# Four scatters of a batch in one run ahead of the masking products, in place of two pairs around them

## What is computed

```python
h = _layernorm(x) * (1 + ca) + sa
x = x + ga * attention(h)          # 16 heads of 8 columns, windows of 64 tokens
h = _layernorm(x) * (1 + cb) + sb
x = x + gb * experts(h)            # 8 experts, hidden 352, the best 2 of each token

# attention: a window of 64 queries sees its own 64 keys (causal) and the 64 before it
scores = einsum('bhcqd,bhckd->bhcqk', qc, kcat) / HD ** 0.5
attn = softmax(where(mask, scores, -inf))
out = einsum('bhcqk,bhckd->bhcqd', attn, vcat) @ w_out
# experts
top_vals, top_idx = top_k(xt @ Wg.T, 2)
y = W2[e] @ (silu(W1[e] @ t) * (W3[e] @ t)), weighted by softmax(top_vals), summed over the two
```

## Time and profile before

| | |
|---|---|
| time, median of 3 runs | 276.14 us (273.75 to 278.57) |
| profiled execution | 275.3 us |
| its span, first to last instruction | 273.1 us |
| granted PE clock, mean over the span | 0.932 of full speed |
| PE busy | 218.6 us (80%), 2696 instructions |
| DVE busy | 166.8 us (61%) |
| ACT busy | 115.3 us (42%) |
| POOL busy | 126.6 us (46%), 125 instructions |
| POOL, scatters into `routed` (L1392) | 32 instructions, 32.4 us |
| POOL, masked keys (L1381) | 7 instructions, 16.2 us |

### The profile page before, as it was taken

One profiled execution on the slowest core, in us unless ns is written; L12 is line 12 of the kernel. 1 busy time (PEld: TensorE's weight loads), 2 busy tenths in 40 slices (PEclk: granted clock), 3 DMA queues, 4 the chain that ended last, 5 costly groups with the idle time before them and its releaser, 6 DMA issues.

```text
span 273.1 us, 7726 instructions
## 1 busy us (share of the span) xinstructions
PE 218.6 (80%) x2696; PEld 149.7 (55%) x2698; DVE 166.8 (61%) x527; ACT 115.3 (42%) x259; POOL 126.6 (46%) x125
## 2 busy tenths in 40 slices
PE   6875998999989899997688875698999999993000
PEld 2442465756546575664456654476778887872000
DVE  4695599998585968858472944633444444442492
ACT  3324455546554544654435331223444444433430
POOL 5727263508549183764224174523444444444251
PEclk9999799999999999999979995979999999999555
DMA  6329900000000010000101121231121111100851
GB/s 185 108 79 431 447 23 2 4 2 22 22 13 29 2 33 12 22 22 13 31 22 58 31 60 48 69 88 59 58 60 57 48 52 43 58 21 31 265 159 38
DMA packets 16488, 19.32 MB, mean 71 GB/s; under 512 B 2578, under 2 KB 14998, under 8 KB 16202
## 3 DMA queue, kind: packets, MB, share of 16 engines
q1 hardware_dynamic: 13786, 14.43, 16.6%
q0 software_dynamic: 2240, 4.28, 4.5%
q10 hardware_dynamic: 432, 0.20, 0.3%
HBM read 13.03 MB, written 6.13 MB: 70 GB/s over the span
## 4 chain that ended last, share of the span: by engine, by line
PE 59%; DVE 16%; DMA 6%; ACT 6%; issue 4%; another core or an unknown queue 2%; POOL 2%; SPq 1%; ACTq 0%; DVEq 0%; POOLq 0%
PE pair L754 9%; PE pair L728 7%; PE pair L730 7%; PE pair L560 4%; PE pair L539 4%; DVE nd L1010 4%; ACT pt L841 4%; PE pair L736 4%; PE pair L504 4%; PE pair L545 3%; PE pair L575 3%; PE pair L476 2%; DVE fin_b L1330 2%; PE pair L534 2%
## 5 line engine op out<-in xcount | busy, mean ns | idle before, releaser
L1440 POOL DMA_INDIRECT ranked<-y_sb,ix_u x36 | 35.4, 984 | 46.5 <-ACT y_sb L930 35.9
L1306 DVE TENSOR_TENSOR gated<-pair,act 128x352 f32<-128x352 f32 x36 | 18.9, 524 | 51.8 <-PE pair L730 41.8
L841 ACT ACTIVATE pt<-pair 128x1024 f32<-128x1024 f32 x32 | 33.0, 1030 | 31.7 <-PE pair L545 31.7
L1010 DVE TENSOR_REDUCE nd<-pair 128x8 f32<-128x1024 f32 x32 | 37.7, 1220 | 9.4 <-PE pair L504 9.1
L1392 POOL DMA_INDIRECT routed<-pay,row_u x32 | 32.4, 1012 | 12.6 <-issue 6.3
L754 PE MATMUL pair<-we_sb,gated_t 128*128 x216 | 31.9, 286 | 0.8 <-ACT y_sb L930 0.8
L728 PE MATMUL pair<-we_sb,x_t 128*128 x72 | 29.7, 495 | 2.8 <-ACT x_t L924 2.8
L754 PEld LDWEIGHTS pair<-we_sb,gated_t 128*128 128x128 f32 x216 | 28.2, 199 | 1.7 <-issue 1.6
L730 PE MATMUL pair<-we_sb,x_t 128*128 x72 | 28.2, 474 | 0.0
L1357 POOL TENSOR_TENSOR rstd<-veps,cf_sb 128x2 f32<-128x2 f32 x8 | 6.0, 748 | 47.5 <-DVE veps L1050 47.5
L914 ACT ACTIVATE act<-pair 128x352 f32<-128x352 f32 x36 | 16.7, 464 | 16.0 <-PE pair L728 16.0
(11 more groups left out here) (167 smaller groups left out, 388.1 us busy)
## 6 DMA issues: line engine op xcount, KB each, us to landing
we_sb<-we SPq DMA_DIRECT2D x1, 4352.0 KB, 18.9
xt_in<-routed SPq DMA_DIRECT2D x36, 64.5 KB
mod_bc<-mod_rows SPq DMA_DIRECT2D x1, 2048.0 KB, 8.7
fin_y<-ranked SPq DMA_DIRECT2D x8, 256.0 KB, 4.7
out<-fin_b SPq DMA_DIRECT2D x8, 128.0 KB, 1.8
x_all<-x SPq DMA_DIRECT2D x1, 768.0 KB, 6.2
ranked<-y_sb,ix_u POOLq DMA_INDIRECT x36
routed<-pay,row_u POOLq DMA_INDIRECT x32
```

What stands on the lines that cost most here:

```text
L841: act.activation(pt[:, 2 * half:2 * half + 2, :].rearrange("p j k -> p (j k)"), src[:, :], ACT.Exp).then_inc(done, 1)
L1010: dve.tensor_reduce(nd[:, :, 2 * half:2 * half + 2, 0].rearrange("p s j -> p j s"), src[:, :].rearrange("p (j s k) -> p j s k", j=2, s=4), ...
L1440: pool.indirect_dma_start(ranked[:, :], bass.IndirectOffsetOnAxis(ap=ix_u[q][:, 0:1], axis=0), y_sb[q][:, :], None, bounds_check=TOPK * TO ...
```

## The change

In iterations 3 to 7 POOL first waits until the scores of unit 2b + 1 are done, then issues all four scatters of batch b - 3, and then does the two masking products. The scatters at the end of the iterations go away, and behind the loop the four scatters of batch 5 go out without a wait on `pv_done`. Nothing else changes; PE, DVE, ACT and SP have the same instructions in the same order.

```diff
             for b in range(B):
+                if b >= 3:
+                    pool.wait_ge(s_done, 2 * b + 2)
+                    rows_chosen(b - 3)
+                    scatter_tile(b - 3, 0)
+                    scatter_tile(b - 3, 1)
                 if b + 1 < B:
                     mask_k(b + 1)
-                if b >= 3:
-                    pool.wait_ge(pv_done, 2 * b)
-                    scatter_tile(b - 3, 1)
-                if b + 1 < B:
                     mask_q(b + 1)
...
                 if b >= 1:
                     inv_std2(b - 1)
-                if b >= 2:
-                    rows_chosen(b - 2)
-                    scatter_tile(b - 2, 0)
                 gate_wout(b)
-            pool.wait_ge(pv_done, G)
+            rows_chosen(B - 3)
+            scatter_tile(B - 3, 0)
             scatter_tile(B - 3, 1)
             inv_std2(B - 1)
```

## The result

The changed kernel takes 302.64 us (median of 4 runs, 301.22 to 305.19), the kernel before beside it 275.41 us: a ratio of 1.104, with a 95% interval of 1.098 to 1.110. I had predicted 276.9 us and no measurable difference. It is slower by about 27 us. The profiled execution took 301.2 us, its span (first to last instruction) 299.0 us against 273.1.

What follows compares the result with a forecast made beforehand. The prediction took a chain on PE, then DVE, to bound each attention period, without POOL. Only L1068's delay counted, 4 x 0.18 = 0.72 us, other terms zero: 276.14 + 0.72 = 276.9 us, range 274.3 to 279.8.

Steps and rivals of the forecast that it cites:

- What bounds the kernel: Attention stage: the chain of a 16.1 us period runs on PE, then DVE; POOL does not stand in it.
- First term: Attention stage: POOL's run of four scatters takes 4.78 us, masked keys and queries still come in time; cost zero.
- My 0.40 us of room: Masked keys end at 103.07, PE's second scores want them at 103.47; less about 0.1 us for the signal.
- Second term: L1363 moves beside DVE's L1068, which takes 0.80 us: +0.18 us passed to PE in four periods, 0.72 us.
- Third term: DVE's L1014 takes 0.19 us again in four periods, but DVE then waits for PE's L575: worth zero.
- Fourth and fifth term: Fourth: masked queries done 0.12 us before DVE's L1087, no stall. Fifth: attention stage's end, loads come later than scatters, zero.
- Rival two: POOL's scatter run exceeds 4.90 us, so late masking products hold DVE's L1087; small form 278.3 us, chance 0.10.
- large form: Each scatter waits for the previous transfer, run 9.6 us, keys 4.2 us late: 292 us; 0.05, shared with a split run.
- five rivals: L1014 gain 270.5 us (0.05), late masks, no cost (0.18), L1068 held for all of L1363 (0.08), run split.
- The chance of 0.06 for slower: Whole kernel slower by more than the 2%, 5.5 us, that a measurement can't tell from no change: chance 0.06.

Runs made afterwards that it cites:

- e11_last_period: Kernel before with only the last attention period's first pair of scatters moved behind L560; ratio 0.998 (0.990 to 1.005) on chip 0.
- e1_after_pv: Changed kernel with the run of four scatters waiting for pv_done instead of s_done; 287.20 us on chip 7, 20.4 us slower than the kernel before.
- e14_two_kinds: Changed kernel with eight plain POOL transfers replacing the run in two periods, scatters there between masked keys and queries; 274.77 us on chip 0.
- e15: Same kernel as e14_two_kinds, run on chip 11; 300.00 us, ratio 1.090 (1.072 to 1.108) against the kernel before.
- e8_two_ahead_b: Changed kernel with two scatters ahead of the masked keys and two between masked keys and queries; 284.18 us on chip 4, +11.4 us.

## Why the prediction was wrong

**What bounds the kernel.** I took POOL to matter only where somebody waits for a result of POOL. That is where it failed: PE waits for no result of POOL in the gaps, and no wait on the trace names POOL. Yet the gaps come where POOL writes scatters and go where it doesn't; that what PE lacks is its own instructions is a reading.

**First term, the scatters and what is behind them: "Cost: zero".** This is the failed step. Its timetable for POOL held: the run began 0.37 us after the scores (0.27), was 4.84 us long (4.78), the keys were never waited for and L1087 kept its 0.16 us. Missing was the term for what a scatter does to the engine beside it: 3.35 us of gaps and 1.56 us at half clock a period, 18.4 us in four periods, and about 9 us more in the two that follow. In the kernel before, the first pair ended 0.4 us after the start of L560 and cost one short gap (1.51 us in place of 1.10), and the second waited for `pv_done`, behind L560. The change put four side by side with PE's densest stretch. That the wait on `pv_done` kept them apart, I did not weigh.

The zero was too low for the keys as well, by a smaller amount. My 0.40 us of room for them are no more than the short gap of the kernel before: without it (e11_last_period, chip 0) PE wants the keys 7.37 us after the first scores, in place of 7.79. On that chip the changed order makes PE wait 0.35 and 0.20 us for them. On a chip with gaps PE comes late itself, and the wait doesn't show.

The hint was in my own rows. In the earlier trace rows L560 stands as a piece of 26 at 129.64 in the chain, while a whole one is 64. It was broken up by "issue" gaps of 0.25 and 0.42 us, beside the one pair of scatters that in the kernel before is still being written 1.2 us after the start of L560. I used that row to time POOL's answer and did not ask why the piece was short. One pair costs 0.67 us of gaps there; four scatters from ahead of L560 cost 2.40 us of gaps (0.45 + 0.43 + 0.43 + 1.09), and 1.3 us after the last of them the clock was at its lower level.

**Second term, L1363 against L1068: +0.18 us.** Right for L1068 and L598, too large for the period. L1068 takes 0.80 to 0.82 us (0.80 predicted) in each of the four, and L598 now starts 0.29 us after the scores, put down to `pay`, where it was 0.10 us before. But L470 and L471 give most of it back: L560 starts only 0.04 us later in its period (the table's first line), so "all of the 0.18 us passes to PE" did not hold. By the Trainium skill, "SBUF — State Buffer", Who interferes with whom, L1068, which issues second, would be held until L1363 ends at 83.78 and last 1.02 us. The 0.82 us measured say no, as the 0.80 us of the earlier trace rows did.

**Third term, L1014: worth zero.** Right as far as these traces tell, since PE is what is late here. It takes 0.19 us, and DVE then waits 9.36 us for L575, in place of 2.72.

**Fourth and fifth term.** L1087 is not stretched, as said. The end of the stage was called zero and lost 8.7 us (5.7 and 3.0). L560 breaks up there too, with no masking product of POOL in the last attention period, so it isn't the masks. How the 3.0 us of the period after it come about was not taken apart.

**The rivals.** Rival two had the right sign, but another mechanism (late keys). In its large form it was priced at 292 us; a run of 9.6 us puts the keys 4.4 us late and not 4.2, which makes it 16 us in place of 15. The changed kernel shows none of it on a chip with gaps; e1_after_pv shows that it exists and costs 20 us where the run starts behind L560. None of my five rivals let POOL act on PE without a wait. The chance of 0.06 for slower was too small for a change that moves 4.8 us of one engine's work beside another's densest stretch.

**What stays open.** How scatters cut PE's supply, why plain transfers don't, and why two of six numbered chips don't show it, no run here tells. That it is PE's supply of instructions is the reading that fits all the rows (no semaphore, independent of operands, a stock and then a slow drip), but nothing in the trace measures what PE's sequencer has at hand. The trace does list the packets that bring instructions: 20 and 10 on two queues in both kernels alike, and none from 86 to 91 us, while the gaps last. So if the supply is cut, it is not seen in these packets. The changed kernel as a whole was not run on a chip without gaps, only its periods in e14_two_kinds.

## What to carry to other kernels

Before moving indirect transfers of POOL, look at what PE does in that time, even when nobody waits for POOL: beside a stretch of many short instructions (here 64 products with 64 loads), keep them away. Behind it they leave it whole, but what waits behind them on POOL then comes late: e1_after_pv pays 20 us for that. A repeated group that stands in the trace in pieces, with "issue" gaps between them, is a cost that already exists in the kernel; look what runs beside it before calling a move free. A gap can also hide in a piece that is merely long (1.51 us in place of 1.10). Compare kernels on one chip: here the changed order costs 4.6 us a period on one and 0.3 to 0.5 us on another.

## What the runs showed of the chip

- While POOL writes indirect scatters (0.96 us each, 0.30 us apart), PE does 1 to 6 products with their weight loads every 0.74 us, mostly with gaps of 0.39 to 0.50 us between them, after 94 to 106 instructions counted from the start of the scatters. The Trainium skill, "Runtime: NRT & Kernel Launch", Instruction fetch mechanics, says that instruction fetch is hidden behind the time to issue. If a lack of instructions is what the gaps are, the trace disagrees; no run here shows that it is.
- Eight plain transfers issued by POOL in 4.4 us do nothing of the kind, nor do transfers issued by SP.
- The runs on chips 4, 5, 6 and 11 show the gaps, those on 7 and 0 do not. The same program (e14, e15) has a span of 270.3 us on chip 0 and 298.7 on chip 11.
- After gaps of 2.40 us between 86.75 and 90.10, PE's clock was at 0.50 (1.2 GHz) from about 91.4 to 94.6. After one gap of 0.41 us in e8_two_ahead_b it stayed at 1.00.
